# First attention of a two-layer kernel: one step of two maxima, scores, a whole value product one step late and scores, in place of two half steps

## What is computed

```python
q = _split(lora_linear(x, Wq, bq, Bq, Aq))      # 4 x 16 heads x 1024 x 16
k = _split(lora_linear(x, Wk, bk, Bk, Ak))
v = _split(lora_linear(x, Wv, bv, Bv, Av))
scores = jnp.einsum('bhqd,bhkd->bhqk', q, k) * SCALE
attn = jax.nn.softmax(scores, axis=-1)
out = jnp.einsum('bhqk,bhkd->bhqd', attn, v)
out = out.transpose(0, 2, 1, 3).reshape(B, L, H * hd)
return lora_linear(out, Wo, bo, Bo, Ao)
```

## Time and profile before

| what | us |
|---|---|
| median of 3 runs | 3091.6 |
| lowest and highest run | 3080.47, 3095.89 |
| the profiled execution, its own time | 3078.77 |
| its span | 3077.0 |
| TensorE busy in the span | 2951.5 (96%) |
| VectorE busy | 2102.8 (68%) |
| ScalarE busy | 1852.0 (60%) |
| GpSimd busy | 1019.7 (33%) |
| first attention, from its first exponentials (680.6) to its last bank copied out (1429.6) | 749.0 |

### The profile page before, as it was taken

How to read it: one execution, slowest core, us unless ns; L and a number is a source line. 1 busy time by engine, 2 the same in 40 slices (tenths; PEclk the granted TensorE clock), 3 DMA queues, 4 the chain that set the end, 5 groups by cost and what they waited for, 6 DMA issues and landing times. The chain is left out here.

```text
span 3077.0 us, 66534 instructions
## 1 busy us (share of the span) xinstructions
PE 2951.5 (96%) x23638; PEld 2231.5 (73%) x23638; DVE 2102.8 (68%) x5890; ACT 1852.0 (60%) x4638; POOL 1019.7 (33%) x1627
## 2 busy tenths in 40 slices
PE   7999999999999999998898999999999999999998
PEld 5888888864444444444787888788887888788886
DVE  5666666689999999994765565655556555665556
ACT  4666666658877777775445555455554555545553
POOL 0000000001100000001005666576665766667663
PEclk9999999999999999999999999999999999999999
DMA  4111111231332323301415545454453555355442
GB/s 154 49 49 49 49 49 42 63 70 33 83 46 57 50 36 66 50 6 38 151 45 142 115 112 116 111 139 108 112 130 99 133 118 114 81 127 123 111 111 72
DMA packets 360644, 262.23 MB, mean 85 GB/s; under 512 B 213116, under 2 KB 295676, under 8 KB 360188
## 3 DMA queue, kind: packets, MB, share of 16 engines
q1 hardware_dynamic: 360316, 257.98, 34.6%
HBM read 100.85 MB, written 44.04 MB: 47 GB/s over the span
## 5 line engine op out<-in xcount | busy, mean ns | idle before, releaser
L1007 ACT ACTIVATE a_pt<-ps 128x512 f32<-128x512 f32 x1024 | 556.1, 595 | 170.6 <-PE ps L1043 169.6
L176 DVE TENSOR_REDUCE mx<-ps 128x2 f32<-128x1024 f32 x512 | 622.0, 1224 | 50.0 <-PE ps L167 34.9
L1847 ACT ACTIVATE b_pp<-b_pp,b_nm 128x192 f32<-128x192 f32 (+2 forms) x1024 | 472.8, 463 | 279.3 <-DVE b_nm L2025 209.4
L1817 POOL TENSOR_SCALAR b_pp<-b_pp,b_rc 128x192 f32<-128x192 f32 x960 | 389.3, 428 | 283.6 <-DVE b_rc L2034 283.6
L797 DVE SCALAR_TENSOR_TENSOR f_yac<-ps,f_cw,f_yac 128x128 f32<-128x128 f32 x992 | 278.1, 344 | 125.3 <-PE ps L596 123.0
L2046 DVE COPY b_pt<-ps 128x320 f32<-128x320 f32 (+2 forms) x336 | 166.3, 509 | 276.7 <-PE ps L1941 263.1
L596 PEld LDWEIGHTS ps<-w,f_sq 128*128 128x128 f32 x2048 | 265.2, 191 | 26.5 <-issue 6.0
L2025 DVE CUSTOM_DVE_ANT_0 b_pp<-ps,b_mk 128x192 f32<-128x192 f32 x480 | 170.0, 354 | 158.0 <-PE ps L1919 158.0
L596 PE MATMUL ps<-w,f_sq 128*128 128x128 f32 x2048 | 270.2, 275 | 0.3
L1976 PE MATMUL ps<-b_wo,b_oT 128*128 128x256 f32 x1024 | 241.2, 379 | 0.0
L1056 PE MATMUL ps<-a_pt,a_v 128*32 128x256 f32 x3072 | 239.3, 391 | 0.0
(11 more groups left out here) (291 smaller groups left out, 7817.8 us busy)
## 6 DMA issues: line engine op xcount, KB each, us to landing
b_rt<-b_qf SPq DMA_DIRECT2D x1024, 64.0 KB, 2.0
qk_parts<-f_aa SPq DMA_DIRECT2D x32, 512.0 KB, 2.7
b_vs<-b_vv SPq DMA_DIRECT2D x120, 128.0 KB, 2.9
b_vb<-b_vv SPq DMA_DIRECT2D x120, 128.0 KB, 3.0
b_vs<-b_vv SPq DMA_DIRECT2D x120, 112.0 KB, 2.8
v_rows<-f_va_ SPq DMA_DIRECT2D x16, 512.0 KB, 2.8
rl<-in_W1vT SPq DMA_DIRECT2D x32, 256.0 KB, 3.3
b_wo<-in_W1oT SPq DMA_DIRECT2D x16, 512.0 KB, 3.8
```

The source lines that it names most:

```text
L176: e.tensor_reduce(M["mx"][kh % 3][:, :, jt, h], P.pair(s), AX.X, ALU.max, negate=True).then_inc(P.free_sem(s), 1)
L1007: e.activation(pt[(4 * i + 2 * j + a) % 12][:, :], P.ap((*s, a)), ACT.Exp).then_inc(P.free_sem((*s, a)), 1)
L1817: m = e.tensor_scalar(x, x, r[:, 2 * u + h:2 * u + h + 1], 1.0, ALU.mult, ALU.mult)
L1847: e.activation(x, x, ACT.Exp, bias=nm[n % 4][:, c:c + 1], scale=-1.0, accum_out=sm[n % 4][:, c:c + 1]).then_inc(exp_done, 1)
```

## The change

The two half steps of a step are put together. A step used to be maximum, scores of two heads, the second half of the value product of the step before, maximum, scores of the other two heads, the first half of this step's own value product. It now is two maxima, scores, both halves of the value product of the step before, scores. A third maximum, which a step of the filling phase has, comes ahead of the second scores, where the side entries are too. The copy of bank 7 thereby comes one step later.

```diff
+    def values(i):
+        nonlocal p, side
+        u, h, c = i // 16, i // 8 % 2, i % 8
+        p += [("pv", i, 0), ("pv", i, 1)]
+        if c == 7:
+            p.append(("evac", i // 8))
+            if u % 4 == 3:
...
     for i in range(16 * units):
...
-        p += ahead(2 * i + 1)
+        maxima = ahead(2 * i + 1) + ahead(2 * i + 2)
+        third = [j for j, s in enumerate(maxima) if s[0] == "max"][2:3]
+        cut = third[0] if third else len(maxima)
+        p += maxima[:cut]
         if i + 1 < 16 * units:
             p.append(("score", i + 1, 0))
-        if c:
-            p.append(("pv", i - 1, 1))
+        if i:
+            values(i - 1)
         if side and (2 <= c <= 5 or c and i >= 16 * units - 8):
             p.append(side.pop(0))
-        p += ahead(2 * i + 2)
+        p += maxima[cut:]
         if i + 1 < 16 * units:
             p.append(("score", i + 1, 1))
-        p.append(("pv", i, 0))
-        if c == 7:
-            p += [("pv", i, 1), ("evac", i // 8)]
...
+    values(16 * units - 1)
     return p + side
```

More of the change, by code:

```diff
@@ L853, in first_attention_plan @@
     side = []
+    def values(i):
[5 more added lines that the diff above has]
+            if u % 4 == 3:
+                if i + 1 == 16 * units:
+                    p += side
+                    side = [("last",)]
+                f0 = 8 * (u // 4) + 4 * h
+                for n in range(6):
+                    side += [(s, f0 + n - lag) for lag, s in ((2, "three"), (1, "two"), (0, "one")) if 0 <= n - lag < 4]
     for i in range(16 * units):
```

## The result

The changed kernel takes 3103.17 us (median of 9 runs, 3099.32 to 3114.15), the kernel before 3081.06 (9 runs, 3077.82 to 3095.89). The ratio is 1.0071, with a 95% interval of 1.0057 to 1.0084. The profiled execution has a span of 3101.4 us where it was 3077.0, 24.4 more.

A forecast was written before the change was run, and what follows sets the result against it. The bound was the score loop, no score entry within 1.25 us of another, equal to TensorE's list. Terms 10.8 + 11.9 + 3 made 26 us longer: 3105 for the profiled execution, median 3117, range 3095 to 3138.

The forecast's parts named there:

- From the first scores to the second: Between a step's two score entries, now holding the whole value product: 1.47 us, set by TensorE.
- From the second scores to the first: To the next step's first scores, across two maxima: 1.25 us, set by the bank's release, TensorE idle 0.56 us.
- TensorE's waits in it: Sign in the changed trace: TensorE waits for exponentials some 0.5 us in most steps, 100 us and more in total.
- Does VectorE keep up: VectorE's reductions of maxima: 2.26 us of work in a 2.72 us step, no wait outlasting TensorE's 0.56 us idle.
- waits at the second maximum: Sign against the forecast: a wait at the second maximum of the pair in most steps.
- The turning of the rows: Once a half unit, behind the second scores: the next scores follow at 1.65 instead of 1.25, costing 0.40 us.
- The copy of bank 7: Between the exponentials of the two score entries: makes the following loop 1.34 instead of 1.25, costing 0.09 us.
- Half units: Eight steps of 2.72 plus rows and copy: 22.25 us (before 21.35); with side entries 24.94 (before 24.28).
- 12 half units without side entries: Half units between the first and last but one copy of bank 7: 0.90 us longer each, 10.8 in sum.
- 18 half units with side entries: Three groups of six half units with side entries: 0.66 us longer each, 11.9 in sum.
- the rest: Last two half units about 1 us each, filling phase 1 us: together 3 us longer.
- The faster rival: Loop between second and first scores is shorter with maxima behind it: 28 us less, 3063 us; chance 0.07.

The follow-up runs named there:

- experiments with one part alone: Against the kernel before: only the two maxima put together, value product still in halves, 3147.73 us; only the value product made whole, a maximum ahead of each score entry, 3166.38 us.
- the kernel without ScalarE's wait: Kernel before the change, without ScalarE's wait for the value product of three steps before: 3078.11 us, ratio 0.9986.
- The changed order without ScalarE's wait: Changed kernel, without ScalarE's wait for the value product of three steps before: 3100.67 us, ratio 1.0068 to the kernel before.
- with four banks the changed order: Changed kernel, each maximum made of one head only, the bank so freed given to the scores (four instead of three): 3007.54 us.
- the two orders with three banks: Changed kernel and kernel before, each maximum made of one head only, scores keeping three banks: 3158.35 us (changed) and 3154.08 us (before).
- the old order with four: Kernel before the change, each maximum made of one head only, the bank so freed given to the scores (four instead of three): 3074.83 us.

## Why the prediction was right

The direction and the mechanism came out, and the size too, in part by luck: 26 us were forecast on the profiled execution, 24.4 measured, with terms that missed in both directions. 3117 us was forecast for the median, 36 above what the kernel before then ran at, because the three runs at hand had their median at 3091.6 and nine runs have it at 3081.06. The measured 3103.17 lies in the range.

- *From the first scores to the second*, forecast 1.47: 1.45 (1014.61 to 1016.06). Right.
- *From the second scores to the first*, forecast 1.25: 1.25 (1013.36 to 1014.61). Right, and shown to be the loop: one more bank makes it 0.58, and 0.06 us more in the loop makes it 0.06 longer. TensorE's waits in it were forecast at 0.5 us in most steps, 100 us and more in total; the rows have 63.9 us in 193 waits, 0.33 each, because the matmuls of the maxima are still in flight for part of the gap.
- *Does VectorE keep up*: yes, outside the filling phase; relieved of nearly all of its reduction work it leaves the half unit as it is. Its waits for maxima more than doubled, to 71 us, and cost nothing there. The waits at the second maximum which I had named as a sign against me do occur (1013.95, 0.29 us); weight loads of maxima wait for VectorE 127 times, 32.0 us in total. In the steps shown they end before the score's own wait does, so that sign was badly chosen.
- *The turning of the rows*, forecast 0.40: the step from 1010.29 to 1013.36 takes 3.07, 0.37 more than 2.70. Right in size but not in its way: the first maximum follows the rows in 0.21 us, not 0.52, because it does not wait for VectorE there; the scores follow 1.50 us after the ones before, not 1.65; and the gap behind them is 1.57 instead of 1.45. Here too 0.12 us moved from one gap to the next, as in the experiments with one part alone.
- *The copy of bank 7*, forecast 1.34 for the loop in which it falls: 1.34. It moved by one score entry, half a step; that it comes one step later, as said ahead of the prediction, is wrong.
- *The kernel before*: its quiet half unit was read as 20.0 us plus the whole value product and the rows. Five of its intervals are 1.32 us and not 1.25, some 0.35 us in all, and the kernel without ScalarE's wait has them back. As the forecast started from the measured 21.35, this did not touch the sum.
- *Half units*: 22.25 forecast and 22.09 measured, 24.94 and 24.77. The steps' 0.02 us makes this up; the four side entries were forecast at 2.69 us and take 2.68. So the differences are 0.74 and 0.49 us instead of 0.90 and 0.66.

The sum can be laid beside the two traces half unit by half unit, by the starts of the 32 exponentials of each:

| term of the sum, us | forecast | measured |
|---|---|---|
| 12 half units without side entries | 10.8 | 6.3 |
| 18 half units with side entries | 11.9 | 8.8 |
| the rest | 3 | 9.2 |
| sum | 26 | 24.3 |

Of the twelve, six lie in the filling phase and lost only 1.6 us together; at 0.90 each they were forecast at 5.4. The half unit before the last is both among the twelve and in the rest, and so was counted twice. *The rest* is the term that was mis-sized: the first half unit takes 6.0 us more than before, the last 4.2, and the stage starts 1.1 earlier. Too much in the middle and too little at the ends nearly cancel.

Part of what the ends lost is the clock. It was granted at 0.70 between 676 and 716 us, where it had been 0.85 between 676 and 710, and at 0.93 between 1429 and 1454, where the same end of the stage had 1.00. The changed order without ScalarE's wait has 17 us of low clock at the start instead of 24, and none at the end; there the first half unit takes 3.7 us more than before and the last 2.8. So at the end 2.8 of the 4.2 us are the order's. At the start the two are not told apart.

*The faster rival* named the right thing that would decide, the loop between the second and the first scores. The Trainium skill, TensorEngine Tiling (Array Packing), Key Properties, says that a change of the tiling mode drains TensorE. The traces agree that there is a gap at each change of layout, and that half of those ahead of value products are gone (478 to 265). But the 0.65 us a step, 5.2 a half unit, that the prediction worked out for a pair of gaps did not come, even with the loop out of the way: with four banks the changed order gains 1.49 us a half unit, and a step of 2.14 stands against two half steps of 1.24, 0.34 less. The prediction's comparison of whole lists, 2.16 against 2.50, has this right.

## What to carry to other kernels

A shorter list of instructions on a busy engine is worth only what the loop beside it lets through. Where entries of one kind hand a small ring of buffers back and forth with another engine, measure the least interval between two of them (here in the stretch where no maxima were left) and look at how much of the first engine's other work stands in each interval; work packed unevenly loses by the fullest interval and gains nothing in the emptiest. Add up whole periods rather than single gaps: a weight load that ran 0.12 us further ahead of its matmuls made one gap 1.37 instead of 1.25 and the one before it shorter by as much. To profit from an order with fewer changes of layout, first widen the ring or shorten its loop; and put odd entries where the interval still has room.

## What was not expected of the hardware

With half maxima the granted clock was 0.50, the lower of its two levels, for 198 and 280 us from the start of the stage in the two orders with three banks, and in the old order with four it was 0.66 between 690 and 780 us. In the kernels as built it is 0.85 (before) and 0.70 (changed) for the stage's first 35 to 40 us and 1.00 in the 50 us after them; in no kernel with all its matmuls did the lower level at the stage's start last more than 45 us. In the kernels with half maxima TensorE used one row half instead of two for each maximum. That this is the reason is not shown, and the changed order with four banks, which leaves out the same, had the lower level for only 38 us at the start. With three banks the whole runs were over 70 us slower than the kernel before, while their later half units were shorter (old order) or as long as in the kernel as built (changed order). A time of a kernel that leaves out matmuls says little without the clock beside it.

An exponential of one column takes 0.17 us by its row and lengthens ScalarE's list by 0.06 us only, since it starts before the one ahead of it has ended.
